# Moving the first half's output projection, x1, norm and turn of h2 from the layer stage into the second scan, and taking the diagonal matmuls out of that scan

## The reference, cut to what matters

```python
# scan: 1024 channels, DS = 16 states each, 1024 steps
dA = jnp.exp(d_t[..., None] * A)
state = state * dA + (d_t * u_t)[..., None] * B_t[:, None, :]
y_t = jnp.einsum('ben,bn->be', state, C_t)
...
# layer on the chosen rows
attn_out = jnp.einsum('hst,thd->shd', att, v).reshape(S, N_HEADS * HEAD_DIM) @ wo
x1 = x + attn_out
h2 = _rms_norm(x1, ln2_w)
mlp = jax.nn.silu(h2 @ w_gate) * (h2 @ w_up) @ w_down
processed = x1 + mlp
gated = gate * processed + (1.0 - gate) * x
```

## Time and profile before

| what | value |
|---|---|
| times of the runs | 2831.01, 2834.7, 2835.09 us; median 2834.7 |
| the profiled execution | 2834.77 us, its span 2833.0 us |
| PE busy in the span | 2541.2 us (90%) |
| DVE busy | 1963.8 us (69%) |
| ACT busy | 1614.7 us (57%) |
| POOL busy | 1614.6 us (57%) |
| mean granted TensorE clock | 0.96 of full speed |

### The profile page before, as it was taken

How to read it: one execution, slowest core, us unless ns; L and a number is a source line. 1 busy time by engine, 2 the same in 40 slices (tenths; PEclk the granted TensorE clock), 3 DMA queues, 4 the chain that set the end, 5 groups by cost and what they waited for, 6 DMA issues and landing times. The chain is left out here.

```text
span 2833.0 us, 38276 instructions
## 1 busy us (share of the span) xinstructions
PE 2541.2 (90%) x13528; PEld 1845.5 (65%) x13528; DVE 1963.8 (69%) x2505; ACT 1614.7 (57%) x3478; POOL 1614.6 (57%) x898
## 2 busy tenths in 40 slices
PE   8969999899899649897999999998997799999998
PEld 3346666666666427555888888887763586578853
DVE  5679999999999766535999998998996644110000
ACT  4578887878887443335887877887772214210000
POOL 1269899999999510004899999999992100000000
PEclk9989999999999859998999999999998899999999
DMA  7732242332422497843335335235217741244442
GB/s 274 254 90 83 74 146 70 123 113 68 141 76 68 153 382 266 285 151 129 105 103 159 105 105 169 93 105 186 93 53 283 286 152 49 89 156 151 154 152 101
DMA packets 249629, 410.43 MB, mean 145 GB/s; under 512 B 50656, under 2 KB 134624, under 8 KB 246624
## 3 DMA queue, kind: packets, MB, share of 16 engines
q1 hardware_dynamic: 235936, 351.88, 38.1%
q10 hardware_dynamic: 12160, 51.39, 4.6%
q0 software_dynamic: 1344, 4.72, 0.4%
HBM read 324.04 MB, written 83.89 MB: 144 GB/s over the span
## 5 line engine op out<-in xcount | busy, mean ns | idle before, releaser
L696 POOL TENSOR_TENSOR s_x<-s_hp,k_bC 128x1024 f32<-128x1024 f32 x288 | 680.1, 2367 | 48.9 <-DVE s_hp L1152 48.8
L677 POOL TENSOR_TENSOR s_x<-s_du,k_bB 128x1024 f32<-128x1024 f32 x254 | 600.6, 2376 | 13.9 <-DVE s_du L1178 7.6
L803 PE MATMUL s_py<-k_ident,s_x 128*128 128x128 f32 x4096 | 525.1, 274 | 31.1 <-POOL s_x L696 31.0
L803 PEld LDWEIGHTS s_py<-k_ident,s_x 128*128 128x128 f32 x4096 | 462.7, 142 | 46.5 <-POOL s_x L696 42.7
L1076 ACT ACTIVATE s_pA<-s_delta,k_negA 128x512 f32<-128x512 f32 x512 | 333.6, 681 | 172.4 <-DVE s_x L1129 166.9
L1822 PE MATMUL l_p<-l_hT,l_ring 128*128 128x256 f32 x1792 | 389.7, 381 | 1.9 <-ACT l_hT L1928 1.0
L1822 PEld LDWEIGHTS l_p<-l_hT,l_ring 128*128 128x128 f32 x1792 | 342.2, 191 | 49.2 <-issue 1.4
L1076 ACT ACTIVATE s_x<-s_delta,k_negA 128x512 f32<-128x512 f32 x512 | 340.2, 710 | 0.0
L1152 DVE TENSOR_TENSOR_SCAN s_hp<-s_x,s_carry,s_pA 128x512 f32<-128x512 f32 x256 | 321.6, 1267 | 21.8 <-PE s_pA L785 16.1
L977 ACT ACTIVATE s_xT<-s_duT,k_BT 128x128 f32<-128x128 f32 x1024 | 336.4, 389 | 0.1
L1152 DVE TENSOR_TENSOR_SCAN s_hp<-s_x,s_pA 128x512 f32<-128x512 f32 x256 | 309.9, 1211 | 33.8 <-ACT s_x L1076 22.1
(11 more groups left out here) (218 smaller groups left out, 3718.9 us busy)
## 6 DMA issues: line engine op xcount, KB each, us to landing
k_bC<-scratch_xd SPq DMA_DIRECT2D x32, 1024.0 KB, 10.4
scratch_ug<-p_ug ACTq DMA_DIRECT2D x16, 1024.0 KB, 4.2
k_u<-scratch_ug SPq DMA_DIRECT2D x64, 256.0 KB, 3.2
k_bB<-scratch_xd SPq DMA_DIRECT2D x32, 512.0 KB, 7.4
s_gy<-scratch_ug SPq DMA_DIRECT2D x64, 256.0 KB, 4.4
s_xt<-in_x SPq DMA_DIRECT2D x64, 256.0 KB, 4.7
scratch_x<-s_xt SPq DMA_DIRECT2D x64, 256.0 KB, 2.8
r_x<-scratch_x SPq DMA_DIRECT2D x32, 512.0 KB, 10.3
```

The source lines that it names most:

```text
L677: pool.tensor_tensor(out=x[:, 4 * g:4 * g + 2], in0=du[:, s % 2:s % 2 + 1].broadcast_to([P, 2, HALF]), in1=bB[:, 2 * g:2 * g + 2], op=ALU. ...
L696: pool.tensor_tensor(out=x[:, 2 * i:2 * i + 2], in0=hp_of(s, i), in1=bC[:, 2 * i:2 * i + 2], op=ALU.mult).then_inc(pool_hc, 1)
L803: last = nc.tensor.matmul(py[:, a], x[:, n, a * P:(a + 1) * P], ident[:], is_transpose=True, start=False, stop=n == NS - 1 and a == HALF / ...
```

## The change

In the first layer stage PE, ACT, DVE and POOL stop after the attention. SP stores `base0` (rows that need the attention part added) and the new `hid0` (the residual rows) instead of `h2T0`, and issues all its loads for the second scan right after the last weight tile of the value projection. The attention output `o` stays in SBUF.

In the second scan the fill becomes: 32 matmuls of the output projection for the left 512 columns (`wo`, each second step), DVE adds them to `hid` (x1) and to `base`, three slots later the same for the right columns, then over 13 slots the squares, norm, turn and scaling of h2, then gate, up and down as before. `FILL` gives 26 steps a unit. With the numbers filled in: the output projection runs from unit 0 to slot 1 of unit 5, gate and up from slot 6 of unit 6, down from slot 6 of unit 26, and the last step falls 7 steps before the end of unit 31.

In the second scan pairs 1 and 5 have no matmuls with diagonals any more: POOL makes their delta·u·B too (quads of 4, 2, 4 and 2 states), ACT writes their exponentials to `pA` behind `release`. POOL multiplies only pairs 1, 5 and 7 by C and DVE the five others, in all units. The first scan's tables stay as they are; its diagonals now lie at the end of `bB`.

```diff
+TURNED, SCALED = (3, 7), {0: (1, 5), SPAN: ()}
+
+
+def states_by_pool(first):
+    return [n for n in range(NS) if n // 2 not in TURNED + SCALED[first]]
+
+
+def quad_place(first, g):
+    mine = states_by_pool(first)
+    quad = [n for n in mine if n // 4 == g]
+    return mine.index(quad[0]), len(quad)
...
+    if first:
+        return (1, 5, 7)
...
-FILL = (1, 5, 3, 3, 1, 2, 2, 4)
+FILL = (1, 5, 4, 3, 3, 3, 3, 4)
...
+TILES_WO = H2 * NH // 2
+TILES_UP = TILES_WO + 2 * NI
+TILES_ALL = TILES_UP + NI // 2
+WO_PART = 2 * NH * SPAN
+WO_DONE_0 = fill_slot(WO_PART - 1)
+WO_FROM = (0, fill_from(WO_DONE_0 + 3))
+WO_DONE = (WO_DONE_0, fill_slot(WO_FROM[1] + WO_PART - 1))
+X1_LAG, BASE_LAG = 1, 2
+SQUARE_AT, MEAN_AT, POW_AT, NORM_AT = (WO_DONE[1] + k for k in (4, 4, 5, 8))
+TURN_AT, SPREAD_AT = (WO_DONE[1] + 8, WO_DONE[1] + 10), (WO_DONE[1] + 10, WO_DONE[1] + 12)
 GATE_UP = 2 * NI * KT
-TILES_UP, TILES_ALL = 2 * NI, 2 * NI + NI // 2
...
+                if k < TILES_WO:
+                    h, j = k // (NH // 2), k % (NH // 2)
+                    src = t["wo"][2 * j * P:(2 * j + 2) * P, h * HALF:(h + 1) * HALF].rearrange("(a p) c -> p a c", p=P)
+                    sp.dma_start(ring[:, k % RING].rearrange("p (a c) -> p a c", c=HALF), src).then_inc(w_in[k % RING], 16)
...
-                sp.dma_start(h2T[:].rearrange("p k r -> p (k r)"), t["h2T0"]).then_inc(h2_in, 16)
-                sp.dma_start(coef[:], t["coef0"]).then_inc(coef_in, 16)
...
+                sp.dma_start(hid, t["hid0"].rearrange("(a p) c -> p a c", p=P)).then_inc(hid_in, 16)
+                sp.dma_start(base, t["base0"].rearrange("(a p) c -> p a c", p=P)).then_inc(base_in, 16)
+                sp.dma_start(coef[:], t["coef0"]).then_inc(coef_in, 16)
+                sp.dma_start(ln2[:], t["cols"][:, NH + 2 * NKV + KT:]).then_inc(ln2_in, 16)
...
+                into, n = quad_place(first, g)
                 if s:
-                    pool.wait_ge(summed, after_sum(s - 1, 2 * g))
-                pool.tensor_tensor(out=x[:, 4 * g:4 * g + 2], in0=du[:, s % 2:s % 2 + 1].broadcast_to([P, 2, HALF]),
-                                   in1=bB[:, 2 * g:2 * g + 2], op=ALU.mult).then_inc(w_ready, 1)
+                    pool.wait_ge(summed, after_sum(s - 1, (4 * g + n - 1) // 2))
+                pool.tensor_tensor(out=x[:, 4 * g:4 * g + n], in0=du[:, s % 2:s % 2 + 1].broadcast_to([P, n, HALF]),
+                                   in1=bB[:, into:into + n], op=ALU.mult).then_inc(w_ready, 1)
...
+            def wo(h, k):
+                head, a = k // SPAN, k % SPAN
+                tile = h * NH // 2 + head // 2
+                if k == 0 and h:
+                    pe.wait_ge(x1_ready, SPAN * h)
+                    pe.wait_ge(base_ready, SPAN * h)
+                if k % (2 * SPAN) == 0:
+                    pe.wait_ge(w_in[tile % RING], 16 * (tile // RING) + 16)
+                last = nc.tensor.matmul((p_gate, p_up)[a][:], o[:, head, a * P:(a + 1) * P],
+                                        ring[:, tile % RING, head % 2 * HALF:(head % 2 + 1) * HALF], start=head == 0, stop=head == NH - 1)
+                if k % (2 * SPAN) == 2 * SPAN - 1:
+                    last.then_inc(w_used, 1)
+
+            def turn_h2(j):
+                if j == 0:
+                    pe.wait_ge(x1_ready, SPAN * H2)
+                    pe.wait_ge(base_ready, SPAN * H2)
+                    pe.wait_ge(normed, SPAN)
+                else:
+                    pe.wait_ge(h2_ready, KT // 2)
+                for c in range(KT // 2 * j, KT // 2 * (j + 1)):
+                    for b in range(SPAN):
+                        at = c % 2 * ROWS + b * P
+                        last = nc.tensor.transpose((p_gate, p_up)[c // 2 % 2][:, at:at + P], normed_rows[:, b, c * P:(c + 1) * P], ident[:])
...
-                make_b(s, 1)
+                if 1 in from_pe:
+                    make_b(s, 1)
...
+            def square(b):
+                act.wait_ge(x1_ready, SPAN + b + 1)
+                nc.scalar.activation(normed_rows[:, b], hid[:, b], ACT.Square, accum_out=squares[:, b:b + 1]).then_inc(sq_ready, 1)
+
+            def norm(b):
+                act.wait_ge(pow_ready, 1)
+                nc.scalar.activation(normed_rows[:, b], hid[:, b], ACT.Copy, scale=squares[:, b:b + 1]).then_inc(normed, 1)
+
+            def spread(j, i):
+                act.wait_ge(h2_turned, j + 1)
+                act.wait_ge(ln2_in, 16)
+                act.wait_ge(base_out, 16)
+                for c in range(KT // 2 * j + 2 * i, KT // 2 * j + 2 * i + 2):
+                    nc.scalar.activation(h2T[:, c], (p_gate, p_up)[c // 2 % 2][:, c % 2 * ROWS:(c % 2 + 1) * ROWS], ACT.Copy,
+                                         scale=ln2[:, c:c + 1]).then_inc(h2_ready, 1)
...
+            def add_attention(h):
+                if h == 0:
+                    dve.wait_ge(hid_in, 16)
+                dve.wait_ge(w_used, (h + 1) * NH // 2)
+                for b in range(SPAN):
+                    nc.vector.tensor_tensor(halves(hid[:, b], h), halves(hid[:, b], h), (p_gate, p_up)[b][:], ALU.add).then_inc(x1_ready, 1)
+
+            def add_to_base(h):
+                if h == 0:
+                    dve.wait_ge(base_in, 16)
+                    dve.wait_ge(coef_in, 16)
+                for b in range(SPAN):
+                    nc.vector.scalar_tensor_tensor(out=halves(base[:, b], h), in0=(p_gate, p_up)[b][:], scalar=coef[:, b:b + 1],
+                                                   in1=halves(base[:, b], h), op0=ALU.mult, op1=ALU.add).then_inc(base_ready, 1)
+
+            def mean_square():
+                dve.wait_ge(sq_ready, SPAN)
+                nc.vector.tensor_scalar(squares[:], squares[:], 1.0 / DI, RMS_EPS, ALU.mult, ALU.add).then_inc(mean_ready, 1)
+
...
+                sp.wait_ge(hid_ready, SPAN)
+                sp.dma_start(t["hid0"].rearrange("(a p) c -> p a c", p=P), hid[:]).then_inc(out_done, 16)
+                keep.load_units(sp, t, SPAN, kept)
+                keep.load_delta(sp, t, SPAN, kept)
+                for g in range(NS // 4):
+                    keep.load_states(sp, t, SPAN, g, kept)
+                sp.wait_ge(qk_ready, QK)
+                sp.dma_start(t["k0"].rearrange("p (k r) -> p k r", r=ROWS), kT[:]).then_inc(out_done, 16)
+                sp.wait_ge(coef_chain, 3)
+                sp.dma_start(t["coef0"], coef[:]).then_inc(out_done, 16)
+                sp.wait_ge(v_act, 2)
+                sp.wait_ge(v_vec, 2)
+                sp.dma_start(t["v0"].rearrange("p (a c) -> p a c", c=DI), v[:]).then_inc(out_done, 16)
...
-            pe.wait_ge(expd, COMBOS)
-            for k in range(NH - APART):
-                pe.wait_ge(o_ready, SPAN * (k + 1))
-                rows_of(T_WO + k, o[:, k], acc, k == 0, False).then_inc(w_used, 1)
-            for a in range(SPAN):
-                for k in range(NH - APART, NH):
...
```

294 lines of the change are left out of this document (176 added, 118 removed).

## The result

| kernel | median | lowest to highest | ratio to before, 95% interval |
|---|---|---|---|
| before | 2831.01 us (5 runs) | 2829.24 to 2835.09 | |
| changed | 2816.93 us (5 runs) | 2813.76 to 2819.77 | 0.9947 [0.9932, 0.9961] |

The change makes the kernel 0.53% faster, some 14 us between the medians; 2816 was forecast, the range was 2792 to 2842. The profiled execution took 2814.96 us, its span is 2813.1 us.

What follows compares the result with a forecast made beforehand. The fullest engine sets each unit's length; DVE was to replace PE as the second scan's bound, POOL 1% behind. From 2834.8 us, 65.3 saved in the layer stage and 47.3 added by the scan gave 2816; range 2803 to 2829, all cases 2792 to 2842.

Steps and rivals of the forecast that it cites:

- Part 1: End of the first layer stage: only a barrier of 1.3 us stays after the attention, 65.3 us saved.
- rival 4: Burst of stores and loads reaches into the attention, or the barrier waits for v0: 10 us lost, 2827 us; chance 0.08.
- Part 2: PE in the second scan: 119 us of diagonals leave, 57 come in, 718 us busy; no longer the bound.
- Rival 5: PE's clock drops in the units without fill and at ring waits: +20 us, 2836 us; chance 0.05.
- the rule against the change: Second scan: transposes don't count as busy for PE's clock, so PE would run at 1.2 GHz for 1.6 units without fill.
- Part 3: DVE in the second scan: 53.3 us more multiplications by C and 5.5 of additions, 823.7 us busy.
- Part 4: POOL in the second scan: +148.5 us of delta·u·B, -111.4 of products with C, 816 us at most.
- Part 5: DVE's idle time in the second scan: 57 us, making the scan 881 us, 47 more than before.
- the steady state: Second scan: DVE waits 0.7 to 0.8 us a unit, 24 us, the middle between 8 and 46.
- rival 2: DVE runs like other bounds, steady idle time 8 to 12 us: scan +28, 2798 us; chance 0.15.
- Rival 1: Second scan: POOL and PE hold each other up, 1 us a unit more than forecast, 2848 us; chance 0.10.
- rival 3: Second scan: the ring starves, with late tiles in other units too: +16 us, 2832 us; chance 0.12.

Runs made afterwards that it cites:

- move only: The changed kernel with the second scan's old tables, diagonals for pairs 1 and 5 included: 2811.17 us, ratio 0.9912.
- tables only: The kernel before with only the second scan's tables changed; output projection and fill stay as before: 2866.37 us, ratio 1.0113.
- all of it: The changed kernel with pair 5's diagonals kept, POOL multiplying pair 3 by C, swish and B loads earlier, ring tiles first: 2785.90 us, ratio 0.9833.
- one pair of diagonals: The changed kernel, but pair 5 keeps its diagonals in the second scan and POOL multiplies pair 3 by C again: 2795.06 us, ratio 0.9868.
- the three mended: The changed kernel with B loads issued earlier, the ring's tiles issued first and sigmoid and swish one slot earlier: 2804.45 us, ratio 0.9901.

## Why the prediction was right, step by step

The ways in which the change gains and loses were forecast as they came: a layer stage 65 us shorter, a second scan longer by DVE's new work and its idle time. That 2816.9 came out for 2816 is luck. A gain of 18.0 us was forecast from a base of 2834.8; the medians show 14.1, and the median of before is 3.8 us lower than that base.

**Part 1** holds to 0.2 us, the barrier too (1.12 for 1.3). The burst of moved DMAs cost nothing that shows; rival 4 did not happen.

**Part 2** was wrong by 36 us, which mattered little, since PE was not the fullest engine; at the start of the down projection alone a slow PE may have cost time. The new work is 49 us instead of 57 (move only). What brings PE to 754 is the clock: with the tables only PE has 704 us where 779.7 - 119 = 661 was expected, 43 more at a clock of 0.93. Rival 5 placed the low clock in the slots without fill and at the ring. It is there in part (0.89 from 1400.00 to 1463.70, not half speed throughout), but those 63.7 us hold 7 of the some 53 us of clock that the scan lacks (an estimate: 0.11 of 63.7, 0.06 of 889). Much of the rest follows PE's waits for the recurrence: in the changed kernel the six waits of 2.9 to 3.8 us ahead of the products of pairs 3 and 7 were followed by transposes at half speed (eight in 1.92 to 1.97 us, once seven in 1.76), those of at most 2.1 us by eight in 1.09 or 1.10. In the kernel with all of it there is a slow group after a shorter wait (1.91 us after 1.58) and a fast one after a wait of 2.51, so the length of a wait alone doesn't decide it. One row of each kernel:

```profile
1653.61 1.97 PE L864 MATMUL s_pA<-k_ident,s_xT 128*128 128x128 f32 x8 [2.91 <-DVE s_hp L1292]
```

```profile
1487.97 1.91 PE L867 MATMUL s_pA<-k_ident,s_xT 128*128 128x128 f32 x8 [1.58 <-DVE s_hp L1295]
```

The changed kernel's stretch without fill also bears on the rule against the change. PE's timeline there, transposes alone:

```profile
1405.87 1.09 PE L911 MATMUL s_p_gate<-k_ident,t_hidden 128*128 128x128 f32 x4 [5.23 <-ACT t_hidden L1153]
1406.74 1.06 PE L911 MATMUL s_p_up<-k_ident,t_hidden 128*128 128x128 f32 x4
1407.60 1.92 PE L864 MATMUL s_pA<-k_ident,s_xT 128*128 128x128 f32 x8
1409.30 1.91 PE L884 MATMUL s_py<-k_ident,s_x 128*128 128x128 f32 x8
1412.16 0.63 PE L834 MATMUL s_pm<-k_ident,s_gy 128*128 128x128 f32 x4 [0.94 <-issue]
...
1413.06 1.04 PE L884 MATMUL s_py<-k_ident,s_x 128*128 128x128 f32 x8
```

The transposes ran at half speed behind a wait of 5.23 us and at full speed from 1412.16 on, with nothing but transposes in between. The Trainium skill ("TensorE: Matmul & The Clock Gate", Part 4: PE-mode transpose) says that transposes don't count as PE-busy the same way and that the full clock doesn't engage for them. This trace does not agree: the clock rose behind transposes alone.

**Part 3** (DVE 823.7, measured 822.7) and **Part 4** (POOL 816 at most, measured 797) hold. POOL's is lower since the diagonals were 9.8 us of its work and a quad of four states takes 4.52 instead of twice 2.32. That PE is no longer the bound is shown by one pair of diagonals: PE up, the scan 26 us shorter. That DVE is the bound fits its busy time in both directions (down 31 us there, up 53 with the tables only), but the edits moved POOL's work and the places too.

**Part 5** gave 57 us of idle time, and it is 66.4. The two ends are 15.0 (7.3 + 7.7; 15.4 forecast), `bC` 6.2 (7.8). The term that was sized worst is the one on chunk starts: "it waits 3 to 5 us more at each of three starts, of which DVE, a quad behind, sees perhaps 1: 3 us". POOL waited 5.1 to 8.2, and DVE saw 9 to 11 us of it over the three; with the ring's 4 us and the swish these places hold 15.5 us (889.1 - 873.6, the three mended; 12.5 between the medians) where 7 were forecast. A second term was missing: the start of the down projection, 6.5 us, which the sum doesn't have. The remaining 23 us are the steady state and the norm, for which 27 stood. Two terms too low by 15, the others too high by 6: the 9 us that the idle time is over, and with it the scan (+55.4 for +47.3). The steady state is a remainder here and was not measured by itself. The reason for leaning to its middle failed: with PE relieved, DVE's gate did not wait less for PE's sums than before but more (24.1 for 19.4), and units took 27.1 us from gate to gate, where about 26 stood. Two sums of this part are also off on paper: steady idle time of 8 with nothing else new gives 15.4 + 7.8 + 8 = 31, not 35, and rival 2's 8 to 12 with the other terms kept gives a scan 31 to 35 us longer, not 28.

**The sum.** The medians' gain is 14.1 us, which is 65.5 - 55.4 = 10.1 and a rest of 4 that lies within what runs of one kernel differ by (before: 2829.24 to 2835.09). The profiled executions' 19.8 holds 9.7 from stages that were costed at nothing.

**Rival 1** (POOL and PE hold each other up) was not the likeliest, but its mechanism is what the chunk starts show: POOL late, PE's sums late, DVE's gate late. It needed a cause from outside, the late `bB`. Rival 2's scan of 862 did not come, and of rival 3 only the two waits of PE for the ring, 3.7 and 3.3 us, which were in the forecast.

What stays open: why the fullest engine keeps 48 to 54 us of idle time in six of these kernels, with whatever engine it is. The ends and `bC` explain some 21 of it. In the kernel with the three mended 10 more are DVE's gate at the start of the down projection (6.0) and in the last unit (4.1).

## What to carry to other kernels

When three engines are within 3% of each other, take work off the fullest one only as far as the next: here the move alone gained more than the move with PE's relief, and half the relief gained more than either.

A table of who does what is also a table of who waits for whom. The same 1.1 us of work cost 3 us a unit in one slot and under 1 in another, and two steps of fill moved by one slot cost 34 us, at that slot and at the start of the down projection. Look at each moved piece for the instruction behind it in the same queue and the same banks, before counting busy time.

In a full pipeline a late load at a chunk's start is absorbed only in part by the engine that waits for it: here DVE felt about half. Issue what is already free ahead of SP's next wait.

A scan's length from one execution can mislead by 5 us. Two gains that don't seem to add up may add up between medians.

## What the runs showed of the hardware

- An engine that is relieved can get slower: with 119 us of full-speed work less, PE was busy only 76 us less (779.7 to 704.2, tables only), since its granted clock fell from 0.98 to 0.93. The scan had 54 us over its fullest engine in both, so no cost of it shows where PE was not the bound.
- The granted clock can rise behind transposes alone: half speed at 1409.30 (eight in 1.91 us), full speed from 1412.16 on (four in 0.63, eight in 1.04), in the changed kernel.
- POOL's multiplication of 2048 columns takes 4.52 us and two of 1024 take 4.71.
